# A bidirectional LSTM feeding a deformable convolution: DMAs on SyncE's queue carry rows in and states out of the recurrence's buffers

## The reference, cut to what matters

```python
x = x + _L0_conv_ref(_gn(x), ...)   # group norm, then an LSTM along f, both ways, and a linear layer
x = x + _L1_conv_ref(_gn(x), ...)   # a 3x3 convolution and two deformable ones, fused by a 1x1
```

```python
gx = jnp.einsum('nfc,gc->nfg', y, W_ih) + b_ih + b_hh
def step(carry, g_in):
    h, c = carry
    i, f, gg, o = jnp.split(g_in + h @ W_hh.T, 4, axis=-1)
    c = sigmoid(f) * c + sigmoid(i) * tanh(gg)
    h = sigmoid(o) * tanh(c)
    return ((h, c), h)
```

## Time and profile before

| | |
|---|---|
| median of 3 runs | 845.68 us (842.84 to 846.45) |
| the profiled execution's own time | 846.11 us |
| its span, first to last instruction | 844.2 us |
| busy: TensorE matmuls | 729.8 us, 86% |
| busy: VectorE | 612.0 us, 73% |
| busy: ScalarE | 492.6 us, 58% |
| busy: GpSimd | 259.6 us, 31% |
| the recurrence | 38.4 to about 204 us of the span |

### The profile page before, as it was taken

How to read it: one execution, slowest core, us unless ns; L and a number is a source line. 1 busy time by engine, 2 the same in 40 slices (tenths; PEclk the granted TensorE clock), 3 DMA queues, 4 the chain that set the end, 5 groups by cost and what they waited for, 6 DMA issues and landing times.

```text
span 844.2 us, 61069 instructions
## 1 busy us (share of the span) xinstructions
PE 729.8 (86%) x27570; PEld 590.9 (70%) x27570; DVE 612.0 (73%) x1126; ACT 492.6 (58%) x1008; POOL 259.6 (31%) x284
## 2 busy tenths in 40 slices
PE   0589999999689999587779999999999999999970
PEld 0355555557258899432469999999989999999960
DVE  4466666665812322568758999999999999999975
ACT  0344444443332432366658888878878887888854
POOL 1122222210000000000224445454465656656533
PEclk9999999999879999789999999999999999999995
DMA  9200000000000000000000000000000000000006
GB/s 238 89 2 2 0 0 0 0 2 1 4 3 4 5 4 4 4 1 1 3 4 0 0 0 0 0 0 0 0 0 0 0 0 0 0 0 0 0 2 199
DMA packets 4062, 12.04 MB, mean 14 GB/s; under 512 B 1391, under 2 KB 1787, under 8 KB 3460
## 3 DMA queue, kind: packets, MB, share of 16 engines
q1 hardware_dynamic: 1716, 4.88, 2.1%
q10 hardware_dynamic: 1522, 4.21, 1.8%
q0 software_dynamic: 768, 2.10, 0.9%
HBM read 6.99 MB, written 4.19 MB: 13 GB/s over the span
## 4 chain that ended last, share of the span: by engine, by line
PE 66%; DVE 17%; ACT 8%; issue 5%; DMA 2%; POOL 2%; ACTq 0%; DVEq 0%; POOLq 0%
PE psum L1022 17%; PE psum L951 16%; PE psum L898 13%; PE psum L977 8%; PE psum L969 5%; DVE wide L608 5%; DVE wide L611 4%; ACT wide L423 4%; ACT wide L419 3%; PE psum L921 2%; DVE offs L696 2%; DMA xs<-in_x_dram 2%; DVE stats L643 1%; POOL out_dram L254 1%; DVE xs L652 1%
## 5 line engine op out<-in xcount | busy, mean ns | idle before, releaser
L509 ACT ACTIVATE wide<-psum 128x512 f32<-128x512 f32 x576 | 301.5, 600 | 15.1 <-PE psum L951 8.1
L951 PE MATMUL psum<-wide,sels 125*32 125x256 bf16 x4608 | 231.9, 275 | 3.1 <-issue 2.5
L1022 PE MATMUL psum<-wide 128*32 128x64 f32 x8192 | 194.9, 220 | 3.4 <-issue 3.4
L720 DVE TENSOR_SCALAR wide<-wide 128x1024 f32<-128x1024 f32 x256 | 180.2, 724 | 2.8 <-ACT wide L509 2.6
L1022 PEld LDWEIGHTS psum<-wide 128*32 128x32 f32 x8192 | 169.6, 110 | 5.2 <-issue 3.9
L727 DVE COPY wide<-psum 128x1024 f32<-128x1024 f32 x128 | 156.1, 1219 | 2.0
L359 POOL COPY wide<-offs 125x256 bf16 (+1 forms) x64 | 28.7, 449 | 389.3 <-DVE offs L696 212.7
L351 POOL TENSOR_SCALAR wide<-wide 128x512 f32<-128x512 f32 x64 | 135.9, 2123 | 7.2 <-ACT wide L509 7.2
L898 PE MATMUL psum<-img,offs 32*32 32x512 f32 x3456 | 112.3, 610 | 5.8 <-ACT img L451 5.8
L977 PE MATMUL psum<-wc,wide 32*64 32x128 f32 x4096 | 112.7, 283 | 1.3 <-issue 1.3
L816 PEld LDWEIGHTS psum<-wide 128*64 128x64 f32 x2048 | 70.3, 137 | 61.0 <-DVE wide L619 60.0
(11 more groups left out here) (101 smaller groups left out, 772.8 us busy)
## 6 DMA issues: line engine op xcount, KB each, us to landing
xs<-in_x_dram ACTq DMA_DIRECT2D x8, 256.0 KB, 10.7
xs<-in_x_dram SPq DMA_DIRECT2D x8, 256.0 KB, 10.1
out_dram<-wide SPq DMA_DIRECT2D x16, 128.0 KB, 3.5
out_dram<-wide POOLq DMA_DIRECT2D x16, 128.0 KB, 4.2
offs<-in_cw_dram ACTq DMA_DIRECT2D x1, 576.0 KB
sels<-in_sel_dram ACTq DMA_DIRECT2D x1, 562.5 KB
wide<-in_dsc_dram ACTq DMA_DIRECT2D x1, 288.0 KB
offs<-in_dwd_dram ACTq DMA_DIRECT2D x1, 288.0 KB
```

Of the source, the lines that this page charges most:

```text
L509: nc.scalar.activation(hat_tile(par, i), use_bank(par, hat_use(i)).rearrange("p (q n) -> p q n", q=2), ACT.Abs).then_inc(d_read, 1)
L720: nc.vector.tensor_scalar(v, v, 1.0, 1.0, ALU.min, ALU.subtract).then_inc(v_ready, 1)
L951: last = mm(bank[c, e * SL:(e + 1) * SL], sels[:, k, c], oc[0:NROW, par, :], start=(e == 0), stop=(e == 1))
L1022: last = mm(ps[O_BANK][C * q:C * q + C, cols], w, v, start=(group == 0), stop=(group == GROUPS - 1))
```

## The change

The copies of `stage_x` and `store_h` on GpSimd go away, with GpSimd's loop. SyncE issues DMAs from one part of the on-chip memory to another in their place, written out for 15 groups: per group two for the rows (each 128 partitions x 2 x 256 elements, 256 KB), one for the forward states (64 partitions x 512 elements, 128 KB) and four for the backward states (64 partitions x 128 elements, 32 KB each, one for each step, since their order is reversed). `xst` is laid out by batch first, as `xg` is; the reversed order of the backward rows is read by TensorE in `gates_x` and no longer made by the copy. `xst_ready` and `h_stored` become one semaphore for each of the two buffers, counted in 16 for a DMA. VectorE's copies of the first group's rows keep their place with plain order. GpSimd clears the border of `pad` as soon as the rows of the last group are used.

```diff
@@ -110,7 +110,7 @@
         hst = region(2 * GROUP * SEQ).rearrange("p (s n) -> p s n", s=2 * GROUP)
-        xst = region(2 * 2 * GROUP * SEQ).rearrange("p (s d f n) -> p s d f n", s=2, d=2, f=GROUP)
+        xst = region(2 * 2 * GROUP * SEQ).rearrange("p (s d b f t) -> p s d b f t", s=2, d=2, b=2, f=GROUP)
         dsc_s = region(2 * K * P)[0:C, :].rearrange("p (a k m) -> p a k m", a=2, k=K)
@@ -161,8 +161,8 @@
         h_ready = [sem(f"h_ready{b}") for b in range(2)]
-        xst_ready = sem("xst_ready"); x_used = sem("x_used")
-        hf_stored = sem("hf_stored"); h_stored = sem("h_stored"); h_last = sem("h_last")
+        xst_ready = [sem(f"xst_ready{par}") for par in range(2)]; x_used = sem("x_used")
+        h_stored = [sem(f"h_stored{par}") for par in range(2)]; h_last = sem("h_last")
         pool_turn = sem("pool_turn")
@@ -188,6 +188,7 @@
         UNROLL = 2 * GROUP
+        STORE = 16 * (1 + GROUP)
@@ -263,6 +264,30 @@
             sp.dma_start(wlin_s, wlin).then_inc(lstm_in, 16)
...
+            def stage_x(group):
+                for d, f0 in ((0, group * GROUP), (1, S - (group + 1) * GROUP)):
+                    sp.dma_start(xst[:, group % 2, d], xg[:, :, f0:f0 + GROUP, :]).then_inc(xst_ready[group % 2], 16)
+            def store_h(group):
+                f0, tile = group * GROUP, hst[:, group % 2 * GROUP:(group % 2 + 1) * GROUP]
+                for b in range(2):
+                    sp.wait_ge(h_ready[b], (group + 1) * GROUP + 1)
+                sp.dma_start(hall[0:DQ, f0:f0 + GROUP].rearrange("p f b t -> p f (b t)"), tile[0:DQ]).then_inc(h_stored[group % 2], 16)
+                for j in range(GROUP):
+                    sp.dma_start(hall[DQ:P, S - 1 - f0 - j].rearrange("p b t -> p (b t)"), tile[DQ:P, j]).then_inc(h_stored[group % 2], 16)
+            sp.wait_ge(xg_ready, 2)
+            stage_x(1)
+            for group in range(NG - 1):
+                if group + 2 < NG:
+                    sp.wait_ge(x_used, group + 1)
+                    stage_x(group + 2)
+                store_h(group)
             sp.wait_ge(lin_ready, NCH)
@@ -291,28 +316,8 @@
             nc.gpsimd.memset(hst, 0.0).then_inc(zeroed, 1)
-            nc.gpsimd.nop().then_inc(h_stored, 2)
-            def stage_x(rows, rows_b, par):
-                nc.gpsimd.tensor_copy(xst[:, par, 0].rearrange("p f (b t) -> p f b t", b=2),
-                                      xg[:, :, rows, :].rearrange("p b f t -> p f b t"))
-                nc.gpsimd.tensor_copy(xst[:, par, 1, ::-1].rearrange("p f (b t) -> p f b t", b=2),
-                                      xg[:, :, rows_b, :].rearrange("p b f t -> p f b t")).then_inc(xst_ready, 1)
-            def store_h(rows, rows_b, par, count, stores, staged):
-                for b in range(2):
-                    pool.wait_ge(h_ready[b], count)
-                pool.wait_ge(xst_ready, staged)
-                pool.sem_inc(pool_turn, 1)
-                tile = hst[:, par * GROUP:(par + 1) * GROUP]
-                nc.gpsimd.tensor_copy(hall[0:DQ, rows].rearrange("p f b t -> p f (b t)"), tile[0:DQ]).then_inc(hf_stored, 1)
-                pool.wait_ge(hf_stored, stores)
-                pool.sem_inc(pool_turn, 1)
-                nc.gpsimd.tensor_copy(hall[DQ:P, rows_b].rearrange("p f b t -> p f (b t)"), tile[DQ:P, ::-1]
-                                      ).then_inc(h_stored, 1)
+            for par in range(2):
+                nc.gpsimd.nop().then_inc(h_stored[par], STORE)
@@ -324,22 +329,6 @@
             halve(wlin_s, 0.5).then_inc(halved, 1)
-            pool.wait_ge(xst_ready, 1)
-            stage_x(ds(GROUP, GROUP), ds(S - 2 * GROUP, GROUP), 1)
-            with pool.Fori(0, NG // 2 - 1) as it:
-                for par in range(2):
-                    pool.wait_ge(x_used, it * 2 + (par + 1))
-                    pool.wait_ge(h_stored, it * 2 + (par + 2))
-                    pool.sem_inc(pool_turn, 1)
-                    stage_x(ds(it * (2 * GROUP) + (par + 2) * GROUP, GROUP),
-                            ds(it * (-2 * GROUP) + (S - (par + 3) * GROUP), GROUP), par)
-                    store_h(ds(it * (2 * GROUP) + par * GROUP, GROUP),
-                            ds(it * (-2 * GROUP) + (S - (par + 1) * GROUP), GROUP), par,
-                            it * (2 * GROUP) + ((par + 1) * GROUP + 1), it * 2 + (par + 1), it * 2 + (par + 3))
-            store_h(ds(S - 2 * GROUP, GROUP), ds(GROUP, GROUP), 0, S - GROUP + 1, NG - 1, NG)
-            pool.wait_ge(h_stored, 2 + NG - 1)
             pool.wait_ge(x_used, NG)
@@ -594,10 +583,8 @@
             dve.wait_ge(xg_ready, 2)
-            nc.vector.tensor_copy(xst[:, 0, 0].rearrange("p f (b t) -> p f b t", b=2),
-                                  xg[:, :, 0:GROUP, :].rearrange("p b f t -> p f b t"))
-            nc.vector.tensor_copy(xst[:, 0, 1, ::-1].rearrange("p f (b t) -> p f b t", b=2),
-                                  xg[:, :, S - GROUP:S, :].rearrange("p b f t -> p f b t")).then_inc(xst_ready, 1)
+            nc.vector.tensor_copy(xst[:, 0, 0], xg[:, :, 0:GROUP, :])
+            nc.vector.tensor_copy(xst[:, 0, 1], xg[:, :, S - GROUP:S, :]).then_inc(xst_ready[0], 32)
@@ -614,7 +601,7 @@
                 if group is not None:
-                    dve.wait_ge(h_stored, group)
+                    dve.wait_ge(h_stored[j // GROUP], group)
                 dve.wait_ge(tc_ready[b], count)
@@ -626,7 +613,7 @@
                 for st in range(UNROLL):
-                    dve_step(st, it * UNROLL + (st + 1), it * 2 + (st // GROUP + 1))
+                    dve_step(st, it * UNROLL + (st + 1), it * STORE + STORE)
@@ -791,18 +778,18 @@
-            def gates_x(b, g, par, group):
+            def gates_x(b, g, par, staged):
                 if b == 0 and g == 0:
-                    pe.wait_ge(xst_ready, group)
+                    pe.wait_ge(xst_ready[par], staged * 32)
                 if g % 2 == 0:
...
                     last = mm(bank[DQ * d:DQ * d + DQ, (g % 2) * GROUP * S:(g % 2 + 1) * GROUP * S], wx_s[:, d, g, :],
-                              xst[:, par, d, :, b * S:(b + 1) * S], start=False, stop=(g % 2 == 1))
+                              xst[:, par, d, b, ::1 - 2 * d, :], start=False, stop=(g % 2 == 1))
                 if b == 1 and g == 3:
@@ -825,19 +812,19 @@
-            def pe_step(j, count, group):
+            def pe_step(j, count, staged):
...
                     gates_h(b, j, count)
-                    if group is not None:
-                        gates_x(b, j % GROUP, 1 - j // GROUP, group)
+                    if staged is not None:
+                        gates_x(b, j % GROUP, 1 - j // GROUP, staged)
             for st in range(UNROLL):
-                pe_step(st, st + 1, st // GROUP + 2)
+                pe_step(st, st + 1, st // GROUP + 1)
             with pe.Fori(1, NG // 2 - 1) as it:
                 for st in range(UNROLL):
-                    pe_step(st, it * UNROLL + (st + 1), it * 2 + (st // GROUP + 2))
+                    pe_step(st, it * UNROLL + (st + 1), it + (st // GROUP + 1))
@@ -853,7 +840,7 @@
             for st in range(GROUP):
-                pe_step(st, S - UNROLL + st + 1, NG)
+                pe_step(st, S - UNROLL + st + 1, NG // 2)
             pe.wait_ge(conv_in, 16 * 7)
@@ -865,7 +852,8 @@
                 taps += 1
-            pe.wait_ge(h_stored, 2 + NG - 1)
+            pe.wait_ge(h_stored[0], (NG // 2 + 1) * STORE)
+            pe.wait_ge(h_stored[1], NG // 2 * STORE)
             pe.wait_ge(h_last, 1)
```

## The result

The changed kernel took 838.58 us (median of 4 runs, 837.54 to 838.89) against 846.07 us before; the ratio is 0.9905, with a 95% interval of 0.9884 to 0.9926. So it is faster, by 7.5 us and not by 13.0, and the time lies 0.6 us above the predicted range of 829 to 838.

The account below looks back on a forecast made before the run. It took the recurrence as bound by a chain through VectorE, lengthened by GpSimd's copies. Removing them saves 13.0 us, the DMAs add 0: 845.7 - 13.0 = 832.7 us, own range 830 to 835, wider range 829 to 838.

Parts of the forecast that it names:

- The transfers are hidden: Each group's seven DMAs: last lands at about 6.8 us, due one group (9.2 us) later, so they cost nothing.
- Rival 1: Each group's start: VectorE and TensorE wait for late transfers; 892 us at a 10.1 us landing. Chance 0.07.
- Rival 3: Recurrence: DMAs lengthen VectorE's instructions as the copies did, gain gone, 842 to 846 us. Chance 0.05.
- rival 4: SP queue works its DMAs off one after the other: 24.5 us a group, over 1,000 us. Chance 0.02.
- Rival 5: Recurrence: TensorE becomes the bound once VectorE no longer waits for copies, 834 to 838 us. Chance 0.04.
- the estimate of about 925 us: Group's seven DMAs run singly by the Trainium skill's fit: 2.1 us per 32 KB store, 15.8 us for all seven.
- the edge of the stage: Recurrence's start: the first two staging DMAs land in time for TensorE's second group; price 0, if last about 3 us.
- Rival 2: Recurrence's start: the first rows land late, once, for 3 us, giving 836 us. Chance 0.07.
- The sum: Loads around the recurrence's start: 1.5 MB plus 0.5 MB more at 229 GB/s take 8.6 us, to 38.6.
- The 13 stores: Recurrence: 7 stores in VectorE's loop body at 0.89 us (6.2) and 6 after its turn at 0.92 (5.5) saved.
- The last store: Recurrence's end: the last two stores, without copies in behind them, save 0.52 us each, 1.0 us together.
- The check by the means: VectorE's three recurrence lines: means less undisturbed times, 128 times their sum, give 13.4 us of lengthening against 13.0.

Follow-up runs that it names:

- e5: Kernel of e2 with the same bytes in 16 DMAs a group instead of 7: 863.70 us, ratio 1.0208.
- e2: Changed kernel with the second layer's seven weight loads issued by SP behind the first two staging DMAs: 835.66 us, ratio 0.9873.
- e1: Changed kernel with the second group's rows copied by GpSimd again, all other groups by DMA: 837.21 us, ratio 0.9884.
- e8: Kernel of e2 with a group's four backward stores as one 128 KB DMA, steps read in reversed order: 835.00 us, ratio 0.9863.
- e9: Changed kernel with only the last weight load, sels, moved to SP behind the first two staging DMAs: 835.77 us, ratio 0.9885.
- e11: The changed kernel measured once more, nothing altered, 6 runs: 835.48 us (833.98 to 842.60), ratio 0.9879.
- e7: Kernel of e2 with VectorE's wait for h_stored moved ahead of the group's first L595: 834.48 us, ratio 0.9865.

## Why the prediction was wrong

**The terms that held.** The copies on GpSimd lengthened VectorE's instructions; with the copies gone, the instructions have their undisturbed means. The transfers are hidden, seven issues and a landing in some 7 us of 9.4 (6.8 of 9.2 was said); e5 found the edge of that cover where the sum put it. They do not slow the engines: 74 GB/s beside the recurrence and L598 at 225 ns. Moving operands with reversed rows cost nothing that the spacing shows. GpSimd's memset costs nothing. Rivals 1, 3, 4 and 5 did not come, nor did the estimate of about 925 us beside rival 4: one 32 KB store landed in 1.9 us, near its 2.1, but seven DMAs took 7 us together and not 15.8, since they overlap. (The Trainium skill, page "DMA: Bandwidth & Descriptors", section "Anatomy of one DMA", gives that fit for DMAs that GpSimd issues; these are SyncE's.)

**The step that failed** is the price of 0 for the edge of the stage: "these two DMAs should land well before the whole". Rival 2 came, with a chance of 0.07 and a price of 3 us, and it cost 4.4 (155.90 against 151.53 us in e2). Two errors are in it. The sum took the bytes ahead and the rate of the whole DMA, 229 GB/s, as if every load used every engine. The rate of the next stretch, 65 GB/s over 5 us, stood there, and its bytes too were priced at 229; it was a load on few engines. And the two input queues that landed alike (10.1 and 10.7 us) carried loads of one shape; `sels` and the staging are not of one shape. The wait itself was 3.0 us, the rival's price. The other 1.4 us fall behind it, mostly where TensorE's clock was granted at 0.50, and the rival's price left that out.

**Terms mis-sized.** I priced each group against 1.15 for all its eight half-steps. One of them is 1.22, for VectorE's wait for h_stored, which the copies' disturbance covered in the profile before. The 13 stores that I priced so were worth 0.07 us less each, 0.9 us together. The last store was worth 0.16 us and not 0.52. It had 1.55 + 1.27 us, and in the changed kernel the same two spacings are 1.14 and 1.52, since the slow pace of the last group now begins one half-step earlier:

```profile
183.99 0.29 DVE L595 SCALAR_TENSOR_TENSOR wide<-wide 128x128 f32<-128x128 f32 x1
...
185.13 0.29 DVE L595 SCALAR_TENSOR_TENSOR wide<-wide 128x128 f32<-128x128 f32 x1
...
186.65 0.29 DVE L595 SCALAR_TENSOR_TENSOR wide<-wide 128x128 f32<-128x128 f32 x1 [0.42 <-ACT wide L408]
```

The two make 1.3 us less, and the other terms came out some 0.2 us larger than priced. So of the 13.0 us 11.9 were there to be had, and e1, e2, e8 and e9 all show them (recurrence of 151.5 against 163.4 us). The check by the means was partly luck: the busy times of the three lines fell by 14.5 us, 109.5 to 95.0, so not all of the lengthening lay on the chain.

Together: 13.0 - 1.1 - 4.4 = 7.5 us, which is what the recurrence lost in the profile. The comparison of the two profiles' spans, 7.3 us, is 0.2 less, by the stretches around it.

**What stays open.** The changed kernel's two measurements, 838.6 and 835.5 us, differ by more than most of what was tried here. Both profiled runs had the wait at the start (3.0 and 2.6 us); whether the others had it can't be read, and five of e11's six runs took 834.0 to 837.9 us, inside the predicted range. So the 4.4 us are shown for the profiled runs, and that they make the median of 838.6 is argued. And why the clock falls at the linear layer in some executions and not in others, the profiles don't tell: TensorE had the same instructions before it in both.

## What to carry to other kernels

Where a copy engine and VectorE both read the on-chip buffer, look at which event releases the copy: here the ones released by VectorE's own result met VectorE's next instructions in every group, and they were the ones to move first. When DMAs take over, count issues against the cover. For the first of them ask what is queued on each DMA engine, not how many bytes are queued in all. When a disturbance goes, a smaller one under it appears, so take the undisturbed pace from the same place of the loop and not from its quiet part.

## What the runs showed that I had not expected

A copy inside the on-chip buffer lands 1.9 us after its issue for 32 KB, 2.2 for 128 KB and 2.6 for 256 KB, with 0.50 to 0.65 us of the issuing engine for each; the landing is below the 3.5 us of the nearest row before. One load of 562.5 KB on 125 partitions delayed a 256 KB copy of another queue from 3.8 to 9.6 us: five engines did all of it, and there its long packets took turns with the copy's short ones. And one satisfied wait in VectorE's program costs 0.07 us on a tight chain, 0.03 more when doubled, and nothing inside the loop's body (0.09 at its turn) when it stands two instructions earlier (e7).
